# A relative-position attention layer: the merge of the two window tiles on VectorE is replaced by matmuls over both tiles

## The reference

```python
x = x + layernorm(attention(layernorm(x)))
x = x + layernorm(layernorm(x) @ (ternary(weight) * alpha).T + bias)
```

```python
idx = clip(key - query, -64, 64) + 64
logits = einsum('bhqd,bhkd->bhqk', q, k) + einsum('bhqd,qkd->bhqk', q, embK[idx])
w = softmax(logits, axis=-1)
out = einsum('bhqk,bhkd->bhqd', w, v) + einsum('bhqk,qkd->bhqd', w, embV[idx])
return out @ Wo.T + bo
```

## Time and profile before

| | |
|---|---|
| median of 3 executions | 2844.18 us (2843.22 to 2847.89) |
| the profiled execution | 2847.89 us |
| its span, first to last instruction | 2846.1 us |
| mean granted TensorE clock | 0.983 of full speed |
| PE busy with matmuls / with weight loads | 2648.1 us / 1971.7 us |
| DVE, ScalarE, GpSimd busy | 2036.7, 1573.9, 1018.2 us |

### The profile page before, as it was taken

The page is one execution under the profiler, slowest core; times in us unless marked ns, Lnnn a source line. Parts: engine busy times, 40 slices in busy tenths (PEclk is TensorE's granted clock), DMA queues, the critical chain, the costliest instruction groups (busy, mean ns, idle before and its releaser), DMA issues.

```text
span 2846.1 us, 102506 instructions
## 1 busy us (share of the span) xinstructions
PE 2648.1 (93%) x43218; PEld 1971.7 (69%) x43218; DVE 2036.7 (72%) x5187; ACT 1573.9 (55%) x2993; POOL 1018.2 (36%) x2275
## 2 busy tenths in 40 slices
PE   5899999999999999999999999999999999999995
PEld 3567777677776777667776777767777677777773
DVE  4776678676786677866787667776677766787774
ACT  3555556455555555555555565545665455565651
POOL 4113333433334333443234442334323433331025
PEclk8899999999999999999999999999999999999997
DMA  8545644446455464555545556446554456445410
GB/s 224 180 127 169 181 140 129 133 144 181 130 149 145 136 169 131 138 153 160 163 118 144 166 148 162 118 122 175 162 147 126 111 173 180 142 127 145 133 43 27
DMA packets 602999, 409.08 MB, mean 144 GB/s; under 512 B 145578, under 2 KB 602282, under 8 KB 602282
## 3 DMA queue, kind: packets, MB, share of 16 engines
q1 hardware_dynamic: 602538, 402.52, 50.1%
HBM read 206.83 MB, written 194.90 MB: 141 GB/s over the span
## 4 chain that ended last, share of the span: by engine, by line
PE 68%; DVE 16%; issue 5%; ACT 4%; POOL 3%; DMA 0%; SPq 0%; DVEq 0%; ACTq 0%; POOLq 0%
PE logitsT L755 14%; PE oacc L793 14%; PE scores L732 14%; PE logitsT L760 6%; DVE maxes L1012 6%; DVE junk L1009 5%; PE misc L856 4%; PE misc L692 4%; PE misc L818 3%; ACT wxr L1212 2%; PE misc L830 2%; PE misc L706 2%; PE misc L806 2%; POOL rs L1245 1%; DVE stats L915 1%
## 5 line engine op out<-in xcount | busy, mean ns | idle before, releaser
L1009 DVE CUSTOM_DVE_ANT_1 junk<-scores,bands 128x512 bf16<-128x512 f32 x988 | 680.2, 688 | 606.7 <-PE scores L732 588.5
L755 PE MATMUL logitsT<-qs,ks 98*128 98x128 bf16 (+3 forms) x9088 | 995.9, 216 | 33.6 <-ACT wxr L1212 24.6
L1212 ACT ACTIVATE wxr<-logitsT 128x512 f32<-128x512 f32 x1024 | 600.8, 602 | 584.6 <-PE logitsT L755 487.8
L755 PEld LDWEIGHTS logitsT<-qs,ks 98*128 98x128 bf16 (+1 forms) x9088 | 679.6, 99 | 272.4 <-issue 101.3
L1212 ACT ACTIVATE wy<-logitsT 128x512 f32<-128x512 f32 x1024 | 586.3, 596 | 432.1 <-PE logitsT L755 422.4
L732 PE MATMUL scores<-ks,qs 101*128 101x256 bf16 (+10 forms) x4096 | 719.3, 291 | 77.0 <-DVE maxes L1012 39.4
L1012 DVE TENSOR_REDUCE maxes<-scores 128x1 f32<-128x512 f32 x1024 | 701.6, 685 | 2.2 <-PE scores L732 2.2
L732 PEld LDWEIGHTS scores<-ks,qs 96*128 96x128 bf16 (+3 forms) x4096 | 299.7, 100 | 263.0 <-DVE maxes L1012 121.3
L760 PE MATMUL logitsT<-ident,bands 128*128 128x128 f32 x2048 | 468.5, 281 | 0.0
L1240 POOL TENSOR_SCALAR rs<-rs 128x1 int32<-128x1 int32 (+1 forms) x224 | 48.3, 216 | 977.8 <-DVE rs L920 975.3
L760 PEld LDWEIGHTS logitsT<-ident,bands 128*128 128x128 f32 x2048 | 292.7, 143 | 32.9
(11 more groups left out here) (136 smaller groups left out, 2678.8 us busy)
## 6 DMA issues: line engine op xcount, KB each, us to landing
bs<-praw SPq DMA_DIRECT2D x256, 512.0 KB, 4.2
bands<-bs SPq DMA_DIRECT2D x224, 512.0 KB, 4.4
ks<-kd SPq DMA_DIRECT2D x64, 384.0 KB, 4.9
qs<-qd SPq DMA_DIRECT2D x112, 192.0 KB
bands<-bs SPq DMA_DIRECT2D x128, 128.0 KB, 3.4
qd<-qparts SPq DMA_DIRECT2D x64, 192.0 KB, 2.8
kd<-kparts SPq DMA_DIRECT2D x64, 192.0 KB, 2.5
qd<-qparts SPq DMA_DIRECT2D x64, 128.0 KB, 2.6
```

Source lines behind the costliest of these rows:

```text
L755: mm = e.matmul(lt[:, c * P + q0:c * P + q1], kk[0:depth, h, kt * P:(kt + 1) * P], qs[i][0:depth, h, q0:q1], start=q0 == 0, stop=not near, ...
L1009: e.tensor_tensor_reduce(junk[:], scores[:, 0:512].rearrange("p (a c) -> p a c", a=2), banded, 1.0, LOWEST, ALU.add, ALU.max, mx[:, h, 0:1 ...
L1212: e.activation(dst, src, ACT.Exp).then_inc(exp_ready, 1)
```

## The change

The merge is taken out. `relative` multiplies both halves of `wx` with tables of their own: the table is now 256 positions wide (`WIN`), of clipped distances, less `embV[0]` throughout. Each matmul becomes two, one for each tile, of which the second adds to the first in PSUM; for queries below 64 the left tile goes first, for the others the right one. In quads that end with tile 0 the second turn leaves out that step (48 moving columns). The weighted sum treats the key tile that the query tile straddles (kt = t) as a left one, so that its rows have 17 columns instead of 18; its key tiles are taken in the order 2, 3, 0, 1; in tile 0, key tile 0 is taken whole; and a zero matmul over 256 columns clears the output in step 6 of each eight, as one over 128 columns does in step 7. The slots of `relative` and `relative_sum` move. `relative` waits for the exponentials instead of the merges, and ScalarE's wait for the finished table goes, since `relbase` is now one row of 16, broadcast, in a place of its own.

```diff
-EXT = 2 * P - 1
+EXT = P + WIN - 1
...
-def value_sides(t, kt):
-
-    if t:
-        return [(0, P, kt >= t)]
-    return [(0, HALF, False), (HALF, P, True)]
...
             at(o + 4.1, "weighted", s, blk, "Y")
-            at(o + 3.5, "merge", s, blk)
...
-                    at(z + 29.6 + 1.5 * part + 0.35 * piece, "relative", quad, part, piece)
+                    at(z + 28.8 + 1.8 * part + 0.45 * piece, "relative", quad, part, piece)
             for blk in range(2):
-                at(z + 33 + 0.5 * blk, "relative_sum", quad, blk)
+                at(z + 32.8 + 0.5 * blk, "relative_sum", quad, blk)
...
-        reltab = sb("reltab", [P, P, D])
-        later = sb("later", [P, P])
+        reltab = sb("reltab", [P, WIN, D])
+        relbase = sb("relbase", [P, D])
...
-        relbase = wxr[:, T * H:T * H + P * D].rearrange("p (n d) -> p n d", d=D)
...
-            for tab, at_ in ((reltab[:], 0), (relbase, EXT * D)):
-                e.dma_start(tab.rearrange("p n d -> p (n d)"),
-                            bass.AP(ext.tensor, at_, [[D, P], [1, P * D]])).then_inc(reltab_in, 16)
+            e.dma_start(reltab[:].rearrange("p n d -> p (n d)"),
+                        bass.AP(ext.tensor, 0, [[D, P], [1, WIN * D]])).then_inc(reltab_in, 16)
...
-                    if kind == "X" and blk == 0 and t == 0:
+                    if kind == "X" and blk == 0 and t in (0, T - 1):
                         pe.wait_ge(band_cleared, 1)
-                        cols = oacc[:].rearrange("p (i q) -> p i q", i=4)[:, s % 2 * 2:s % 2 * 2 + 2, 0:HALF]
-                        e.matmul(cols, zero[:, 0:P], zero[:, 0:P], start=first, stop=True, skip_group_check=True)
+                        cols = oacc[:].rearrange("p (i q) -> p i q", i=4)[:, s % 2 * 2:s % 2 * 2 + 2, 0:P if t else HALF]
+                        e.matmul(cols, zero[:, 0:P], zero[:, 0:2 * P if t else P], start=first, stop=True, skip_group_check=True)
                         first = False
...
-                    turns = [1, 2, 3, 0] if kind == "X" and t else range(4)
+                    turns = [2, 3, 0, 1] if kind == "X" and t else range(4)
...
-                        for q0, q1, right in value_sides(t, kt):
+                        for q0, q1, right in sides(t, kt):
...
-                    pe.wait_ge(merged, 2 * QUAD * (quad + 1))
+                    pe.wait_ge(exp_ready, n("exp_ready", "weights", QUAD * quad + QUAD - 1, HG - 1, "X"))
                     pe.wait_ge(*free)
                     pe.wait_ge(reltab_ready, 8)
+                    wraps = quad % (T // QUAD) == T // QUAD - 1
                     for i in range(8 * part + 2 * piece, 8 * part + 2 * piece + 2):
                         o0 = i % 8 * QUAD * HG * 2
-                        for j in range(4):
-                            q = 32 * j + 2 * i
-                            mm = e.matmul(m[32 * j:32 * j + 32, o0:o0 + QUAD * HG * 2],
-                                          reltab[:, 126 - q:128 - q, :].rearrange("p n d -> p (n d)"),
-                                          wx[:, :, :, P + q:P + q + 2], start=True, stop=True, skip_group_check=True)
+                        for turn in range(2):
+                            for j in range(4):
+                                q = 32 * j + 2 * i
+                                side = turn if j < 2 else 1 - turn
+                                nt = QUAD - 1 if wraps and turn else QUAD
+                                n0 = 126 - q + P * side
+                                mm = e.matmul(m[32 * j:32 * j + 32, o0:o0 + nt * HG * 2],
+                                              reltab[:, n0:n0 + 2, :].rearrange("p n d -> p (n d)"),
+                                              wx[:, 0:nt, :, side * P + q:side * P + q + 2], start=turn == 0, stop=turn == 1,
+                                              skip_group_check=True)
...
-                elif stage == "merge":
-                    s, blk = k
-                    left, right = (wx[:, s % QUAD, HB * blk:HB * blk + HB, x:x + P] for x in (0, P))
-                    mask = later[:].rearrange("p (h q) -> p h q", h=1).broadcast_to([P, HB, P])
-                    dve.wait_ge(table_in, 16 * N_TABLE)
-                    dve.wait_ge(pvX, value["pvX", s, blk])
-                    if tile_of(s):
-                        e.copy_predicated(right, mask.bitcast(I32), left).then_inc(merged, 1)
-                    else:
-                        e.tensor_tensor(right[:, :, 0:HALF], left[:, :, 0:HALF], mask[:, :, 0:HALF], ALU.mult)
-                        e.scalar_tensor_tensor(right[:, :, HALF:P], mask[:, :, HALF:P], 0.0, right[:, :, HALF:P], ALU.is_equal,
-                                               ALU.mult).then_inc(merged, 1)
...
                     if kind == "X":
-                        if s:
-                            act.wait_ge(reltab_ready, 8)
                         if s >= QUAD:
                             act.wait_ge(rel_summed, 2 * (s // QUAD))
...
-                    pool.wait_ge(reltab_in, 32)
+                    pool.wait_ge(reltab_in, 16)
                     pool.wait_ge(exp_ready, 2 * i + 1)
-                    part = slice(16 * i, 16 * i + 16)
-                    e.tensor_tensor(reltab[:, part, :], reltab[:, part, :], relbase[:, part, :],
+                    part = reltab[:, 32 * i:32 * i + 32, :]
+                    e.tensor_tensor(part, part, relbase[:].rearrange("p (o d) -> p o d", o=1).broadcast_to([P, 32, D]),
                                     ALU.subtract).then_inc(reltab_ready, 1)
...
-    cyclic = np.r_[1:2 * MRP + 1, 1:2 * MRP]
-    bases = np.where(np.arange(EXT) < P, 2 * MRP, 0)
+    near = np.clip(np.arange(EXT) - EXT // 2, -MRP, MRP) + MRP
...
-        "extV": np.concatenate([embV[cyclic], embV[bases]]).reshape(-1),
-        "later": (p[:, None] > p).astype(f32),
+        "relbase": embV[0],
+        "extV": embV[near].reshape(-1),
```

More of the change, by code:

```diff
@@ L247 @@
     "DVE": {"v_ready": ("project_v",), "negmax_ready": ("max_reduce",), "nm_ready": ("max_rows",),
-            "rel_ready": ("relative",), "o_added": ("relative_sum",), "merged": ("merge",), "attn_ready": ("out_norm",),
+            "rel_ready": ("relative",), "o_added": ("relative_sum",), "attn_ready": ("out_norm",),
             "lin_ready": ("tail_wo", "tail_ff"), "var_ready": ("statistics", "tail_wo", "tail_norm", "tail_ff"),
@@ L389, in build @@
          o_turned, rows_turned, lin_summed, xnT_ready, far_copied, qf_ready, praw_ready, exp_ready, o_copied, rows_ready,
-         v_ready, negmax_ready, nm_ready, rel_ready, o_added, merged, attn_ready, lin_ready, var_ready, y_normed, x1_normed, z_normed,
+         v_ready, negmax_ready, nm_ready, rel_ready, o_added, attn_ready, lin_ready, var_ready, y_normed, x1_normed, z_normed,
          rstd_ready, x1_ready, z_ready, pvX, pvY, oacc_zeroed, threshold_ready) = signals.values()
@@ L518, in sync_program @@
                 e.dma_start(t_[:], a[name].rearrange("(i p) o -> p i o", p=P)).then_inc(table_in, 16)
-            for t_, name in ((later[:], "later"), (outmap[:], "outbase"), (zbuf[0][:, 0:P], "outleft")):
+            for t_, name in ((outmap[:], "outbase"), (zbuf[0][:, 0:P], "outleft")):
                 e.dma_start(t_, a[name]).then_inc(table_in, 16)
@@ L522, in sync_program @@
                 e.dma_start(t_, a[name]).then_inc(table_in, 16)
-            for t_, name in ((bo, "bo"), (bf, "bf"), (alpha, "alpha")):
+            for t_, name in ((bo, "bo"), (bf, "bf"), (alpha, "alpha"), (relbase, "relbase")):
                 e.dma_start(t_[:], a[name].partition_broadcast(P)).then_inc(table_in, 16)
             ext = a["extV"]
-            for tab, at_ in ((reltab[:], 0), (relbase, EXT * D)):
-                e.dma_start(tab.rearrange("p n d -> p (n d)"),
-                            bass.AP(ext.tensor, at_, [[D, P], [1, P * D]])).then_inc(reltab_in, 16)
+            e.dma_start(reltab[:].rearrange("p n d -> p (n d)"),
+                        bass.AP(ext.tensor, 0, [[D, P], [1, WIN * D]])).then_inc(reltab_in, 16)
             sp.wait_ge(junk_set, 1)
```

## The result

The changed kernel takes 2897.36 us (median of 4 executions, 2896.66 to 2898.2), the kernel before 2845.42 us (4, 2843.22 to 2847.89). The ratio is 1.0182, with a 95% interval of 1.0165 to 1.0200: 52 us slower. The forecast was 2885 us, 41 us above 2844, within 2854 to 2912.

What follows compares the result with a forecast made beforehand. PE, 93% busy, was taken to set the pace, DVE counting only where PE stops. Terms A to G: 75.8 + 7 + 6.6 - 11.6 - 9 - 14 - 13 = +41.8, say +41, against the 2844.18 median: 2885 us, range 2854 to 2912.

Steps and rivals of the forecast that it cites:

- PE sets the pace, and DVE counts only where PE stops: Whole kernel: PE, busy 93%, works in order; at most some 127 us of its stops for DVE can be won.
- A: Relative matmuls (L806) double: 4096 more records at 18.5 ns each, nothing off for 48 columns, +75.8 us.
- B: Relative pieces spread and moved ahead: about 1.5 more breaks in 32 quads at 0.15 us, +7 us.
- C: Weighted sum around tile 0: 16 more zero matmuls of 256 columns at 0.41 us each, +6.6 us.
- D to G: PE's stops for DVE that shrink or go: -11.6, -9, -14 and -13 us.
- D: Relative matmuls (L806) no longer wait for the last step's merge: 31 places at 0.37 us, -11.6 us.
- F: Row-maximum stops earlier in the quad, where one merge fewer frees DVE: 1.7 us a batch, eight batches, -14 us.
- E: Row maxima between the relative pieces: PE's longer work there covers DVE, 1.1 us a batch, -9 us.
- G: Stops just ahead of and behind the pieces: PE comes later, 0.8 us at two places a batch, -13 us.
- PE has room: Rival: added records fall into idle array time and freed DVE wins, -41 us, 2803 us; chance 0.06.
- Little recovered: Rival: stops return at the next row maximum, only L806's wait is won, +78, 2922 us; above +68, chance 0.09.
- A dearer record: Rival: second turn pays for adding onto fresh PSUM, 25% on the doubled records, +61 us; above +68, chance 0.09.

Runs made afterwards that it cites:

- old slots: The changed kernel with its relative stages and their sums in the slots of the kernel before: 2896.8 us (1.0182).
- merge and double: The kernel before, merges and slots kept, with a second, adding matmul after every relative matmul: 2909.3 us (1.0225).
- narrow width: The changed kernel with 16 moving columns in the second relative turn instead of 64 or 48: 2887.6 us (1.0147).
- late norms: The kernel before with the second layer norm's result later in DVE's order, then two more norm operations later too: 2839.0 us and 2837.4 us.

## Why the prediction was right, point by point

**PE sets the pace, and DVE counts only where PE stops.** Shown. The 2 by 2 of merges and second turn, in the old slots: merges off -20, second turn on +65, both +53 (old slots, new sums). DVE lost 174 us of work for those 20.

**A, the doubled records, +75.8.** The mechanism was right, and so was the 18.5 ns, for records of 64 columns. From the first load of a run to the next load of another kind, where nothing was waited for and the clock was 2.4 GHz, 16, 32 and 48 records take 0.42, 0.72 and 1.01 us in the kernel before (medians), and 64 and 96 take 1.31 and 1.90 us with merge and double: 18.5 ns for each record more. (The averages over 16 records, 17.8 ns here and 17.5 before, are a little lower, because the first eight loads of a run start some 7 ns apart.) What was wrong is "I give nothing for that", of the 48 columns: 17.8 ns with 64 throughout and 16.8 with the 48, 8192 x 1.0 = 8 us, so that A was 68. "The loads stay as many" is no argument where streaming takes nearly as long as loading. The end fits: 68 us of records and 15 of supply stops, less 16 by which the waits for DVE fell beyond their ordinary gaps, are 67, and the runs with and without the second turn differ by 66.

The 25 ns of the Trainium skill ("TensorE: Matmul & The Clock Gate", section "Wait — 56ns, not 53.3ns?") do not hold for these records, in four column groups: 12.8 ns at the narrow width.

**B, breaks, +7.** More than forecast: 78 more runs, where I had counted 48. But the old slots, with 140 runs, are no faster, so breaks and what the places give in return seem to cancel; neither was measured alone.

**C, zero matmuls, +6.6.** They take 4.9 us of PE's list. Without them and the other changes in the weighted sum the end came 1.3 us earlier, no more than chance. The term was mis-sized.

**D to G, the stops, -47.6.** D, the wait of L806, went as said. For D and F I had 26 us where the run without merges gave 20, which also holds a part of E. For E and G, which need PE's added work, I had 22: the loads of the relative stage with what follows take 89 us more in the run with merge and double, and its end comes 65 us later, so about 24 us were filled. But the two fill the same stops. Alone they give 65 - 20 = 45 us, together 53, so some 7 us counted in both columns were there once only. (In these 7 are also the new sums, about +1 us, the 48 columns, -8, and 6 us more of supply stops than merge and double has.) Of the 175.2 us of waits for DVE 38 went, where 127 in excess of gaps had been there to be won.

**What was missing.** The supply of instructions, 15.9 - 2.1 = 14 us. No term stood for it, and the row that I had, 340 packets of instructions, gives no sign of it; only its place in the timeline does. My sum of 41, with A smaller by 8, C by 5, the double count of 7 and the supply of 14, comes to 49, against the 52 measured. The 3 us that stay are of the size of what a run can tell, and B and the 26 us of D and F stand in the sum as forecast, though D and F gave 20 at most. That the forecast lay within 11 us was in part luck: a term of 14 us was missing, and errors of both signs, -13 and +21, met.

The clock was no term either. The prediction read rows 1 as full clock between the first and the last slices, but a 9 there is 90% or more: it was 1.2 GHz for 23.9 us of the regular part before and 17.1 after. By the price from the late norms the change gained an estimated 3 us by that.

**The rivals.** "PE has room" is excluded by +65 and +66 for the second turn. "Little recovered" lay closer than its 0.09 said: DVE's 174 us gave 20. "A dearer record" was right in sign for another reason than accumulation: a dense stretch costs more than its records.

## What to carry to other kernels

Moving work from an engine with slack to the one that sets the pace costs nearly its whole price there (65 of some 76 us), and gives back only where the pacing engine stops (20 of 174 us); price both from the stops, and not from busy times, and do not add up what two edits win at the same stop. To price a dense run, take the difference between runs of different length, and look at what narrower records among them change. And before many short instructions are added to an engine, look at how fast it already goes through 256 of them: in this kernel the 256 ahead of a stop had mostly taken 2.3 to 4.0 us without it (8 of 27 had taken 4.5 to 5.6), and the same work in pieces had 15.9 us of stops where in one block it had 63.0. And when a short stop goes, look at the granted clock before the gain is put down to the wait: the 6 us of the late norms were the clock's.

## What the runs showed of the hardware that was not expected

PE can outrun its instructions. Packets of 16 KB come on a queue of their own, 337 to 372 in a run, one for every 256 of PE's instructions. Ahead of the stop that ended at 2521.20 PE had begun the last 256 instructions at 2516.44; the packet came from 2518.76 to 2519.79, and PE went on 1.4 us later. At 1303.25 it was 1298.96, 1300.19 to 1301.89, and again 1.4 us. So 4.3 and 4.8 us passed from entering one 256 to having the next; over all such stops of this run it was 2.5 to 6.5 us. What starts a packet, and why the last one ahead of a stop starts anywhere from 0.4 us before that entry to 3.8 us after it, no run here shows.

Fp32 matmuls of 32 output columns in four column groups follow each other at 12.8 ns a record when half of them have 16 moving columns, and at 17.8 ns when all have 64.

PE stops of 1.57 us, one a batch, were followed within 2 us by a granted clock of 1.2 GHz in five of six places, and without them the clock stayed at 2.4 GHz through the regular part. A batch with the stop and 2.4 GHz throughout takes as long as one without the stop (342.1 us), so what these stops cost was the clock behind them, 1.5 to 2.9 us in a batch. The other places at 1.2 GHz in these runs (two in the kernel before) have no such long stop ahead of them, and what brought them about is open.
